# Four chained graph layers: the row-wise transfer moved from the sums to the selections, and the three message parts added in PSUM

## The reference, cut to what matters

```python
m = relu(x[src] + edge_attr); x = LN(x + (1 + eps) * x + segment_sum(m, dst))     # pass 0
x = x * dinv; x = segment_sum(x[dst], src) ...                                     # passes 1, 2
h = relu(segment_sum(x[src], dst) @ w_rel1 + x @ w_root1 + b1)                     # pass 3
x = LN(x + segment_sum(h[src], dst) @ w_rel2 + h @ w_root2 + b2)                   # pass 4
x = LN(x + relu(segment_sum(w_e * x[src], dst) @ w3 + b3))                         # pass 5
```

## Time and profile before

| | |
|---|---|
| median of the timed executions | 10436.51 us |
| the profiled execution, its own time | 10414.08 us |
| its span | 10412.4 us |
| PE busy | 6955.9 us (67%) in 59989 matmuls |
| PE weight loads busy | 5588.1 us (54%) in 59990 |
| DVE busy | 6952.4 us (67%) in 15309 |
| ACT busy | 3898.3 us (37%) in 9751 |
| POOL busy | 4440.2 us (43%) in 4277 |
| granted TensorE clock, mean | 0.621 of full speed |
| DMA | 2048.13 MB, 197 GB/s |

### The profile page before, as it was taken

The page is one execution under the profiler, slowest core; times in us unless marked ns, Lnnn a source line. Parts: engine busy times, 40 slices in busy tenths (PEclk is TensorE's granted clock), DMA queues, the critical chain, the costliest instruction groups (busy, mean ns, idle before and its releaser), DMA issues.

```text
span 10412.4 us, 220272 instructions
## 1 busy us (share of the span) xinstructions
PE 6955.9 (67%) x59989; PEld 5588.1 (54%) x59990; DVE 6952.4 (67%) x15309; ACT 3898.3 (37%) x9751; POOL 4440.2 (43%) x4277
## 2 busy tenths in 40 slices
PE   9999999997045557555675667456765576555676
PEld 9766666665034445444554455345554455555555
DVE  6544444443488887777667766777757776799874
ACT  0455555554167850066005610264016600344200
POOL 0477777777077227400770057102740076000373
PEclk9855555555555557577766766677667776555565
DMA  8233333333879877688776877688768878255675
GB/s 327 64 88 87 88 89 89 86 87 110 267 226 249 264 252 223 143 289 294 226 200 235 290 241 213 176 295 268 220 148 293 292 221 197 102 195 195 201 220 117
DMA packets 1037429, 2048.13 MB, mean 197 GB/s; under 512 B 354974, under 2 KB 476318, under 8 KB 1036958
## 3 DMA queue, kind: packets, MB, share of 16 engines
q1 hardware_dynamic: 764830, 1267.16, 37.8%
q0 software_dynamic: 242832, 700.42, 25.5%
q10 hardware_dynamic: 29680, 79.57, 2.0%
HBM read 1263.63 MB, written 783.00 MB: 197 GB/s over the span
## 4 chain that ended last, share of the span: by engine, by line
DMA 23%; POOL 21%; PE 18%; issue 17%; DVE 16%; DVEq 3%; ACT 1%; POOLq 0%; SPq 0%; ACTq 0%
POOL edge_rows L446 15%; DMA WORK<-messages_in_parts,source 13%; PE psum L778 6%; DVE WORK L1055 6%; POOL WORK L479 6%; PE psum L797 5%; DMA BIG<-edge_rows 5%; DMA WORK<-parts_by_slot 4%; PE psum L664 3%; DVE WORK L1093 2%; DVE BIG L1086 2%; ACT WORK L585 1%; DVEq L67 1%; PE psum L733 1%; PE psum L783 1%
## 5 line engine op out<-in xcount | busy, mean ns | idle before, releaser
L479 POOL DMA_INDIRECT WORK<-messages_in_parts,source x2220 | 2280.4, 1027 | 4544.1 <-DMA messages_in_parts<-WORK 3763.7
L797 PE MATMUL psum<-WORK 128*128 128x144 bf16 x17760 | 2219.8, 297 | 960.4 <-DMA WORK<-messages_in_parts,source 628.4
L797 PEld LDWEIGHTS psum<-WORK 128*128 128x128 bf16 x17760 | 1806.6, 158 | 1373.0 <-issue 674.8
L446 POOL DMA_INDIRECT edge_rows<-WORK x1664 | 1709.6, 1027 | 862.5 <-issue 857.9
L778 PE MATMUL psum<-BIG,WORK 128*128 x11840 | 1287.8, 277 | 1038.2 <-DVE WORK L1055 601.3
L585 ACT CAST WORK<-psum 128x432 bf16<-128x432 f32 x2960 | 1382.5, 522 | 1415.2 <-PE psum L778 1355.6
L862 DVE TENSOR_TENSOR WORK<-lane_k,slot_part 128x1024 bf16<-128x1024 bf16 x2220 | 1529.6, 690 | 481.9 <-PE psum L797 344.3
L1055 DVE TENSOR_SCALAR WORK<-WORK,here 128x1024 bf16<-128x1024 uint8 x2220 | 1667.8, 751 | 98.4 <-DMA WORK<-parts_by_slot 78.9
L778 PEld LDWEIGHTS psum<-BIG,WORK 128*128 128x128 bf16 x11840 | 1013.5, 121 | 1312.6 <-issue 1308.9
L783 PE MATMUL psum<-BIG,WORK 128*128 x17760 | 957.9, 215 | 839.6 <-DVE WORK L1055 732.9
L783 PEld LDWEIGHTS psum<-BIG,WORK 128*128 128x128 bf16 x17760 | 834.9, 116 | 962.7 <-issue 928.9
(11 more groups left out here) (175 smaller groups left out, 7326.7 us busy)
## 6 DMA issues: line engine op xcount, KB each, us to landing
messages_in_parts<-WORK SPq DMA_DIRECT2D x2220, 288.0 KB
WORK<-parts_by_slot SPq DMA_DIRECT2D x444, 640.0 KB, 4.9
BIG<-edge_rows SPq DMA_DIRECT2D x148, 1040.0 KB
WORK<-blocks_by_edge SPq DMA_DIRECT2D x416, 256.0 KB, 3.5
edge_rows<-BIG ACTq DMA_DIRECT2D x1, 76960.0 KB, 209.9
WORK<-in_edge_attr_dram SPq DMA_DIRECT2D x415, 96.0 KB, 2.2
WORK<-messages_in_parts,source POOLq DMA_INDIRECT x2220, 4.1
edge_rows<-WORK POOLq DMA_INDIRECT x1664
```

Of the source, the lines that this page charges most:

```text
L446: pool.indirect_dma_start(rows_dram, bass.IndirectOffsetOnAxis(ap=at_stage[g][:, j:j + 1], axis=0), row_buf[g][:, j, :], None).then_inc(s_ ...
L479: pool.indirect_dma_start(msg[c].rearrange("p k f -> p (k f)"), None, unit_dram, bass.IndirectOffsetOnAxis(ap=source[d][:, t:t + 1], axis= ...
L797: m = pe.matmul(sum_bank(c), onehot[c % GB][:, :, k], msg[c][:, k, :], start=k == 0, stop=k == K - 1)
```

## The change

`messages_in_parts` becomes twice as long (2 U rows) and is now kept in the order of the sums. In the selections POOL writes each batch by an indirect transfer to the rows in `goal`; units without edges go to a row past U. In the sums SP loads the batches in order. ACT first sets the U rows to zero by one transfer of 2304 bytes per row, behind the fill of `edge_rows`, and POOL waits for it before pass 0. POOL's 370 scatters of unit numbers now stand in pass 0, one ahead of each message scatter, and `stage_two` runs two batches behind the selector instead of one. In the sums PE adds each part on its own, 24 matmuls of 48 columns into the same 48 columns, one batch to a bank of five; `reduce_pair` is gone, and `add_sum` reads PSUM. DVE's sum is written out without a loop, and registers are loaded for 30 batches at a time instead of 10.

```diff
+BLOCKS = 30
-        unit_dram = nc.dram_tensor("messages_in_parts", (U, K * W3), BF16).ap()
+        unit_dram = nc.dram_tensor("messages_in_parts", (2 * U, K * W3), BF16).ap()
...
         def sum_bank(c):
-            return bank[c // 2][:, c % 2 * W3:(c % 2 + 1) * W3]
+            return bank[c % GB][:, 0:D]
...
+                def load_messages(i):
+                    for c in range(RING):
+                        wait_past(sp, s_sum, i * RING + (c - RING + 1 + (q * BATCHES if not isinstance(i, int) else 0)))
+                        sp.sem_inc(s_sp_turn, 1)
+                        sp.dma_start(msg[c].rearrange("p k f -> p (k f)").unsqueeze(1), unit_v[:, ds(i * RING + c, 1), :])\
+                            .then_inc(s_gath[c], 16)
...
             for q, (d, kind) in enumerate(PASSES):
                 if q == 0:
-                    pool.wait_ge(s_mcopied, 1)
+                    pool.wait_ge(s_zeroed, 16)
                 for t in range(BATCHES):
+                    if q == 0:
+                        scatter_units(t)
                     c = t % RING
-                    if t == 0:
-                        for k in range(RING):
-                            pool.wait_ge(s_store[k], 16 * PAIRS * (q + 1))
-                    if t >= RING:
-                        pool.wait_ge(s_sum, q * BATCHES + t - RING + 1)
+                    if kind == "plain":
+                        for b in (1, 2):
+                            pool.wait_ge(s_staged[b], t + 1 + plain_before(q))
+                    else:
+                        pool.wait_ge(s_mid, t + 1 + cut_before(q))
+                        pool.wait_ge(s_low, t + 1 + cut_before(q))
                     pool.indirect_dma_start(
-                        msg[c].rearrange("p k f -> p (k f)"), None, unit_dram,
-                        bass.IndirectOffsetOnAxis(ap=source[d][:, t:t + 1], axis=0)).then_inc(s_gath[c], 16)
+                        unit_dram, bass.IndirectOffsetOnAxis(ap=goal[1 - d][:, t:t + 1], axis=0),
+                        msg[c].rearrange("p k f -> p (k f)"), None).then_inc(s_store[c], 16)
...
+            act.dma_start(zero_v, zeros.bitcast(BF16).unsqueeze(1).to_broadcast([128, BATCHES // 2, 2 * K * W3])).then_inc(s_zeroed, 16)
...
-                        if c % 2 == 0:
-                            wait_past(pe, s_reduced, i * GB + (c // 2 + q * (BATCHES // 2) - (GB - 1)))
+                        wait_past(pe, s_added, n - (GB - 1))
                         for k in range(K):
-                            m = pe.matmul(sum_bank(c), onehot[c % GB][:, :, k], msg[c][:, k, :], start=k == 0, stop=k == K - 1)
+                            for f in range(3):
+                                m = pe.matmul(sum_bank(c), onehot[c % GB][:, :, k], msg[c][:, k, f * D:(f + 1) * D],
+                                              start=k == 0 and f == 0, stop=k == K - 1 and f == 2)
...
-                rounds(pe, PAIRS, select_rows)
+                rounds(pe, BATCHES // BLOCKS, lambda i: select_rows(i * BLOCKS, BLOCKS))
+                select_rows(BATCHES // BLOCKS * BLOCKS, BATCHES % BLOCKS)
...
-                    v.tensor_tensor(o, o, pair_sum[c // 2][:, c % 2, :], ALU.add).then_inc(s_added, 1)
+                    v.tensor_tensor(o, o, sum_bank(t % RING), ALU.add).then_inc(s_added, 1)
...
+                for t in range(BATCHES + LAG):
+                    if t < BATCHES:
+                        wait_past(dve, s_sum, t + (q * BATCHES - (GB - 1)))
+                        equal(onehot[t % GB], lane_mk, slot_part[d][:, t, :]).then_inc(s_oh, 1)
+                    u = t - LAG
+                    if u >= 0:
+                        if u % BLOCKS == 0:
+                            its_block = load_blocks(dve, sum_regs[0:min(BLOCKS, BATCHES - u)], batch_block[d][0:1, u:min(u + BLOCKS, BATCHES)])
+                        add_sum(u, its_block[u % BLOCKS])
```

More of the change, by code:

```diff
@@ L140, in gnn_program @@
         w_s = sb("w_s", [128, BATCHES, K])
-        source = [sb(f"source{k}", [128, BATCHES], I32) for k in range(2)]
+        goal = [sb(f"goal{k}", [128, BATCHES], I32) for k in range(2)]
         target_i = sb("target_i", [128, BATCHES], I32)
@@ L206, in gnn_program @@
         msg = [carve(128, [K, W3], BF16) for _ in range(RING)]
-        pair_sum = [carve(P, [2, D]) for _ in range(GB)]
         select = [s.rearrange("p (k u) -> p k u", k=K) for s in SEL]
@@ L401, in _ @@
                         load_rows(0, s)
-                rounds(sp, PAIRS - 1, lambda i: stores(i, True))
-                stores(PAIRS - 1, False)
+                rounds(sp, PAIRS - 1, load_more)
+                for k in range(RING):
+                    sp.wait_ge(s_store[k], 16 * PAIRS * (q + 1))
+                rounds(sp, PAIRS, load_messages)
             sp.wait_ge(s_res, 1)
@@ L462, in _, with scatter_units @@
             pool.wait_ge(s_filled, 32)
-            for t in range(BATCHES):
+            def scatter_units(t):
                 pool.indirect_dma_start(
@@ L759, in _ @@
             turn_parts(SRC)
-            batch_regs = [pe.alloc_register(f"batch_block{k}") for k in range(RING)]
+            batch_regs = [pe.alloc_register(f"batch_block{k}") for k in range(BLOCKS)]
             for q, (d, kind) in enumerate(PASSES):
@@ L812, in _ @@
             batch_regs = [dve.alloc_register(f"batch_block_v{k}") for k in range(RING)]
+            sum_regs = [dve.alloc_register(f"sum_block_v{k}") for k in range(BLOCKS)]
             done = [0]
@@ L976, in _ @@
             dve.wait_ge(s_found, 2 * PAIRS)
[L977 removed]
+            dve.wait_ge(s_const, 19)
             step(v.tensor_scalar(u_valid, u_dblk, float(NB), None, ALU.is_lt))
             step(v.tensor_tensor(u_shift, u_shift, u_here, ALU.add))
[L980 removed]
+            step(v.tensor_tensor(u_a, u_shift, u_trash, ALU.subtract))
+            step(v.tensor_tensor(u_a, u_a, u_valid, ALU.mult))
+            step(v.tensor_tensor(goal[SRC][:, :], u_a, u_trash, ALU.add))
             step(v.tensor_scalar(u_a, u_shift, 1.0 / T, 0.5 / T - 0.5, ALU.mult, ALU.add))
```

121 lines of the change are left out of this document (42 added, 79 removed).

## The result

The changed kernel takes 11151.11 us (median; 11133.26 to 11184.61), the kernel before 10420.51 us beside it. The ratio is 1.0702, with an interval of 1.0664 to 1.0741: **slower by 7.0%**, where +4.9% (10944 us) had been forecast. The profiled execution has a span of 11131.5 us, 719.1 more than before. On the second of the three chips of the experiments the pair was timed again, with a ratio of 1.0713 (1.0676 to 1.0750).

A forecast was written before the change was run, and what follows sets the result against it. POOL's fetches were taken to bound the sums, PE's register-load holes to slow plain selections, POOL's scatters to bound the ranking. Terms 330 - 92 + 190 + 10 + 70 = +508 on 10414.1, plus 22: 10944 us, +4.9%; range 10600 to 11560.

The forecast's parts named there:

- The sums: Six sums: PE's 24 strided weight loads per batch at 64 ns, 1.56 us per batch, 577 us each, +330 us in all.
- The first rival: Sums: strided weights load as fast as packed ones, 380 us per sum, 9762 us in all; chance 0.10.
- The plain selections: Four plain selections: POOL's scatters set 1.39 us per batch, 514 us each, -92 us in all.
- POOL's and VectorE's conflict: Plain selections: scatters starting just after comparison L1055 take 1.49 instead of 0.96 us; random phase adds 0.10 us per batch.
- My rival of falling into step: Plain selections: POOL locks to DVE's phase, each scatter pays 1.79 us, 662 us per selection, 11536 us in all; chance 0.12.
- The register term: Plain selections: PE's register load keeps 4.5 us but comes every 30 batches; hole falls from 0.45 to 0.15 us per batch.
- Pass 0's selection: Pass 0: two POOL transfers per batch make 2.95 us per batch, 1092 us instead of 908; +190 us with extras.
- Pass 5's selection: Pass 5: DVE stays the bound, POOL's transfer fits into 2.2 us per batch but sometimes stretches L1055; +10 us.
- The zero fill: Start of kernel: zeroing lasts to about 510 us, its part after 360 us slowing the ranking; +70 us.
- the counting stage hides the part up to 360 us: Zero fill: zeroing up to 360 us costs nothing beside the counting stage; only 150 us fall into the ranking.
- The mechanism that I did forecast: Ranking: small pieces wait for zeroing pieces, groups take 8.9 us against POOL's 5.34, for 21 groups; +70 us.

The follow-up runs named there:

- ten registers: Changed kernel with block numbers loaded into registers ten at a time instead of thirty (TensorE in selections, VectorE in sums): 11054.18 us, 1.0614 of the kernel before.
- wide and packed runs: Changed kernel with 8 matmuls of 144 columns per sum batch: 11014.38 us, 0.9345; changed kernel with sum weights read from neighbouring columns: 10623.09 us.
- the control: The changed kernel, unchanged, run again on the second chip: 11154.90 us, 1.0713 of the kernel before.
- The short and the halved comparison: Changed kernel comparing 511 or 512 of 1024 columns: 10913.18, 10867.84 us; with later zeroing, wide sums, ten registers and two 512-column halves: 9892.75 us.
- the direct stores: Changed kernel with SP storing selection messages directly in batch order, without indirect message transfers or reordering: 10865.00 us.

## Why the forecast was right in sign and wrong in its parts

- **The sums** (forecast 577 us each, measured 544). The bound was named rightly: PE never idle, 24 loads per batch, VectorE waiting. The size was off: 532.7 us for 8880 loads with ten registers are 60 ns per load, not 64. The other 11 us are what loads of thirty registers on VectorE cost over loads of ten, a term that I had not written at all. The wide and packed runs confirm the bound: a third of the loads gives 386 us, a packed layout 321 to 325.
- **The first rival, strided loads as fast as packed ones**, was refuted. With count, shape, type and granted clock (0.50) the same, a load and its matmul took 57 ns strided and 39 packed, and the sums became slower instead of falling to 380 us. The Trainium skill, "TensorE: Matmul & The Clock Gate", section "Weight-path perf modes", gives the read pattern of a fast weight load as "4 chunks of 32 columns, packed or strided" and no separate time for the two. Here they differ; whether these loads are of that kind no run shows.
- **The plain selections** (forecast -92, measured +222) are the step that failed. The pace was to be 0.96 + 0.30 + 0.10 + 0.03 = 1.39 us; it was 1.57. The 0.10 for POOL's and VectorE's conflict assumed a random phase and at worst 1.49 us. In fact 116 of the 313 scatters between 6000 and 6500 us of the control take 1.6 to 1.8 us, and in the stretch shown above the mean is 239.35 / 191 = 1.25, so the conflict costs 0.28 per batch. The 0.18 beyond my 0.10 are 67 us per pass, most of the error of 79 (+56 instead of -23); 10 more are the longer end of the selection. The DMA engines, for which I had added 0.03, were 0.75 busy and not nine tenths. The trace of the kernel before already spoke against both numbers of the conflict:

```profile
L464 POOL DMA_INDIRECT unit_rows<-unit_meta,target_i x370: 957/1097/7432, 2884.4 to 3458.4; - x185
```

27 of these 370 scatters took 1.7 to 1.8 us, not 1.49 at worst. Their mean, the 1.194 us that I used for pass 0, is 0.20 above 0.96 even without the three longest, beside one comparison every 2.45 us. My rival of falling into step (1.79, 662 us) is as far off on the other side as my 1.39 (514 us): from the first comparison to the last a pass takes 580 to 584. Against it I had argued that the phase drifts when POOL is slowest. The rival was right that a bad phase comes back, and wrong that it stays. The timeline above shows what I had left out: the full ring stops VectorE and lets it go at the landings, and then its comparisons come in bursts. That this is why the bad phase returns so often is my reading; no run separates it. The short and the halved comparison show the conflict directly: scatters of 1.01 to 1.02 and 0.99 us, selections of 528 to 548. The phase of a scatter against the comparison decides whether it is caught, and the length of the comparison for how long: in the first plain selection, the scatters that start 0.1 to 0.2 us after the start of a comparison of 0.74 us take 1.73 us in the mean, after one of 0.50 us 1.19. The register term fell too: the hole grows from 3.8 to 10.7 us with thirty numbers, it did not keep its 4.5, and that costs 9 to 12 us a pass, part of the pace above.
- **Pass 0's selection** (forecast +190, measured +148). Right in mechanism, as the direct stores show: without message scatters the loss is gone. The pace was 2.83 us per batch instead of 2.95, since here the scatters average 627.82 / 566 = 1.11 us and not L464's 1.194; with 0.30 between them that is 2.82.
- **Pass 5's selection** (forecast +10, measured +27). What was missed is not settled. The direct stores leave 14 us of loss that the scatters do not explain, and ten registers made it 9 us longer instead of shorter.
- **The zero fill** (forecast +70, measured +192). The step that failed is "the counting stage hides the part up to 360 us". I had treated an issue as free; it stood 194.46 us, on the very engine that the counting stage waits for. The mechanism that I did forecast exists, but is out of sight in the changed kernel, where the ranking starts after the zeroing has ended. Once the issue is later it shows: groups of 8.95 us where 8.9 had been worked out, and 27 to 61 us given back on the same chip where 70 had been forecast. That each small piece lets a large one pass is how the 8.9 was worked out; the pace fits it, and no run tests it against another way of sharing the engines.

## What to carry to other kernels

A DMA issue is not free when a large transfer is ahead of it on the same queue: put it behind the engine's urgent work. Before an operation is cut into narrower ones, count what each piece brings along (here a weight load); the change's direct loads, with the wide sums kept, ran faster than the kernel before, 0.9345 on the slow first chip and about 0.98 by estimate on the others. And where POOL's indirect transfers set the pace, look at the length and phase of VectorE's instructions beside them: splitting a 0.74 us comparison in two cost VectorE time and still gained 48 us per plain pass. Measure it stage by stage, though, since in pass 0 the same split cost 110 us.

## What the runs showed of the hardware that I had not expected

- An issue of a transfer of 106560 KB held ScalarE for 194.46 us behind one of 76960 KB, and for 179 to 181 us in the four kernels where it came 19 us later.
- Scatters with 0.30 us between them took 0.97 us beside two comparisons of 0.5 us each and up to 1.75 beside one of 0.74, with VectorE the busier engine in the first case. With the halves 1401 of 1462 start in a phase that is not caught in the plain passes, and in pass 0 197 of 717 are caught for longer than before. What fixes the phase in each stage is not shown, and VectorE's mode is not separated.
- A load of 10 registers on TensorE took 2.2 us in the median and 4.2 at most, one of 30 3.8 and 10.8.
- One chip ran the same row scatters of the ranking in 2.8 ms that others ran in 2.2, with the sums identical (543.7 us on both).
